# A fused attention and mixture-of-experts kernel: attention and experts put into one block, the top-k cut into two halves of 8 batches, and the first expert's weights and first chunk placed inside the last attention passes

## The reference

```python
q = layernorm(x) @ Wq.T; k = ctx @ Wk.T; v = ctx @ Wv.T          # 16 heads of 16
y = softmax(mask(q k^T / 4)) v                                    # causal
x = x + tanh(g_xattn) * (y @ Wo.T + bo)

affinity = softmax(x @ gate_w.T)             # [16, 512, 8 experts]
gating, idx = top_k(affinity^T, 128)         # per batch and expert: 128 of 512 tokens
x_in = x[idx]
h = silu(x_in @ w_gate[e].T) * (x_in @ w_up[e].T)
out = scatter_add(zeros, idx, gating * (h @ w_down[e].T))
x = x + tanh(g_ffn) * out
```

## Time and profile before

| | us |
|---|---|
| median of 3 runs | 1907.35 (1906.61 to 1908.03) |
| the profiled execution's own time | 1905.62 |
| its span (first to last instruction) | 1903.9 |
| start of body 15 (last batch's maxima) to last maximum | 751.87 to 794.9 |
| last maximum to `aff` of batch 15 (the drain) | 794.9 to 844.06 |
| `aff` to the first matmul of the experts | 844.06 to 874.69 |
| first matmul of chunk 3 of expert 0 | 969.09 |
| last matmul | 1891.7 |
| busy share of PE, DVE, ACT, POOL | 93%, 57%, 49%, 49% |

### The profile page before, as it was taken

The page is one execution under the profiler, slowest core; times in us unless marked ns, Lnnn a source line. Parts: engine busy times, 40 slices in busy tenths (PEclk is TensorE's granted clock), DMA queues, the critical chain, the costliest instruction groups (busy, mean ns, idle before and its releaser), DMA issues.

```text
span 1903.9 us, 40685 instructions
## 1 busy us (share of the span) xinstructions
PE 1772.4 (93%) x12902; PEld 1017.8 (53%) x12902; DVE 1079.0 (57%) x3480; ACT 930.5 (49%) x1812; POOL 931.3 (49%) x1026
## 2 busy tenths in 40 slices
PE   3899999999999999935899999999899999999997
PEld 1355555555555555422465656565556565656565
DVE  2778888888888887737634343434343434343431
ACT  2466666666666666632334343434343434343332
POOL 6477777777777776543333232333322323333322
PEclk8899999999999999967999999999999999999999
DMA  5777777777777787347464644556736555555222
GB/s 161 163 172 188 189 188 188 188 188 188 188 188 188 188 189 168 81 132 177 100 132 84 120 98 89 98 90 122 123 61 121 100 89 98 89 97 82 48 34 23
DMA packets 408333, 247.85 MB, mean 130 GB/s; under 512 B 289303, under 2 KB 389759, under 8 KB 408191
## 3 DMA queue, kind: packets, MB, share of 16 engines
q1 hardware_dynamic: 383183, 212.39, 47.7%
q0 software_dynamic: 24576, 33.57, 11.3%
q10 hardware_dynamic: 432, 0.13, 0.0%
HBM read 118.63 MB, written 58.72 MB: 93 GB/s over the span
## 4 chain that ended last, share of the span: by engine, by line
PE 50%; DVE 3%; DMA 1%; issue 1%; ACT 0%; POOL 0%; SPq 0%; POOLq 0%; DVEq 0%
PE bank L1101 11%; PE bank L1102 11%; PE bank L1103 11%; PE bank L1117 6%; PE bank L1119 6%; PE bank L1118 6%; DVE h L1219 0%; DVE h L1222 0%; DVE top_at L1169 0%; ACT h L1147 0%; DVE work L1172 0%; DVE top L1167 0%; DMA rows<-tokens,row_now 0%; DMA out<-y,row_now 0%; POOL out L1067 0%
## 5 line engine op out<-in xcount | busy, mean ns | idle before, releaser
L1067 POOL DMA_INDIRECT out<-y,row_now x128 | 202.5, 1582 | 606.6 <-ACT y L1154 581.7
L681 DVE CUSTOM_DVE_ANT_0 masked<-bank,causal 128x128 bf16<-128x128 f32 (+3 forms) x1024 | 445.6, 484 | 69.1 <-PE bank L453 68.2
L565 ACT ACTIVATE prob<-bank 128x512 f32<-128x512 f32 x640 | 367.6, 596 | 158.1 <-PE bank L473 86.1
L1219 DVE TENSOR_TENSOR h<-bank,silu 128x512 f32<-128x512 f32 x256 | 176.4, 689 | 393.5 <-PE bank L1103 259.8
L1147 ACT ACTIVATE h<-h 128x512 bf16<-128x512 f32 x256 | 161.2, 630 | 345.4 <-DVE h L1219 328.5
L1117 PE MATMUL bank<-downT,h 128*128 128x256 bf16 x1024 | 279.1, 273 | 0.0
L1119 PE MATMUL bank<-downT,h 128*128 128x256 bf16 x1024 | 279.1, 273 | 0.0
L1118 PE MATMUL bank<-downT,h 128*128 128x256 bf16 x1024 | 279.1, 273 | 0.0
L1222 DVE TENSOR_TENSOR h<-h 128x512 bf16<-128x512 f32 x256 | 177.3, 692 | 179.7 <-ACT h L1147 175.5
L453 PE MATMUL bank<-ks,qs 96*128 96x128 bf16 (+3 forms) x1024 | 257.8, 306 | 21.0 <-DMA ks<-k_parts 11.4
L1101 PE MATMUL bank<-tokT,gateT 128*128 128x512 bf16 x512 | 195.0, 381 | 35.7 <-DMA tokT<-rows 28.9
(11 more groups left out here) (141 smaller groups left out, 2702.7 us busy)
## 6 DMA issues: line engine op xcount, KB each, us to landing
...
```

Of the source, the lines that this page charges most:

```text
L565: nc.scalar.activation(prob[:, gr % 2, h0:h0 + nh, POFF[tiles[0]]:POFF[tiles[0]] + w], sc_bank[SC_BANK[k]][:, 0:nh * w].rearrange("p (h w) ...
L681: last = nc.vector.tensor_tensor_reduce(masked[:, (gr * NMAX + k) % 2, part], max_bank[max_at(gr, k)][:, part], causal[:, T - w:T], 1.0, L ...
L1067: nc.gpsimd.indirect_dma_start(out_rows, bass.IndirectOffsetOnAxis(ap=row_now[:, par, c, s:s + 1], axis=0), y[:, c % 2, s, :], None, compu ...
```

## The change

Both parts are put into one block. Buffers are laid out by hand in four regions of SBUF; buffers of the experts lie where attention's inputs, scores and drain buffers were, and waits on the counters of attention (`finished`) stand ahead of their first use. The steps of attention's last bodies carry steps of expert 0 (table `AHEAD`): each engine runs them at that group and unit.

The ranks of a chunk are now 64 of 8 batches instead of 32 of all 16: chunks 0 and 1 take batches 0 to 7 (**half** 0), chunks 2 and 3 batches 8 to 15 (half 1). The top-k of a half is 64 rows of 8 batches by 8 experts, which DVE first copies twice side by side (`two`) so that PE's transposes (`rows`) fill all 128 partitions; `copied` brings them to `work`. Each half has its own 16 rounds on a 128x512 tile, 32 in all. A slice covers 64 ranks.

In the last bodies stand: the load of expert 0's gate and up weights at the start of body 15, with the splits through bodies 15 and 16 and the transposes; rounds 0 to 3 of half 0 in body 15, rounds 4 to 15 in body 16, with two slices, eight gathers and eight token transposes in bodies 16 and 17; and the eight `up` iterations of chunk 0 from late in body 16 to body 17. What follows is `first_expert`: chunks 1 to 3 of expert 0 with the whole top-k of half 1 in chunks 1 and 2, and the first weights of expert 1, whose low parts POOL now computes (`lo_on_pool`). The token transposes of chunks 2 and 3 now stand at the end of the list of the chunk ahead, behind the weights of its iteration 7.

```diff
+AHEAD = {
+    (LAST - 1, 0, 8): e0("two", 0), (LAST - 1, 1, 3): e0("rows", 0) + e0("copied", 0),
+    (LAST, 0, 0): e0("load", 0, "gate") + e0("load", 0, "up") + e0("base", 0),
+    (LAST, 0, 6): e0("round", 0, 0), (LAST, 1, 6): e0("round", 0, 1),
+    (LAST, 2, 6): e0("round", 0, 2), (LAST, 3, 6): e0("round", 0, 3),
+    (LAST, 1, 0): e0("weights", 0, 0), (LAST, 1, 4): e0("weights", 0, 1), (LAST, 1, 8): e0("weights", 0, 2),
+    (LAST, 2, 1): e0("weights", 0, 3), (LAST, 2, 5): e0("weights", 0, 4), (LAST, 2, 9): e0("weights", 0, 5),
+    (LAST, 3, 2): e0("weights", 0, 6), (LAST, 3, 5): e0("weights", 0, 7),
+    (LAST, 3, 0): e0("turn", 0, "gate"), (LAST + 1, 0, 3): e0("turn", 0, "up"),
+    (LAST + 1, 0, 1): e0("round", 0, 4), (LAST + 1, 0, 4): e0("round", 0, 5),
+    (LAST + 1, 0, 7): e0("round", 0, 6), (LAST + 1, 0, 9): e0("round", 0, 7),
+    (LAST + 1, 0, 10): e0("slice", 0) + e0("columns", 0) + [p for s in range(4) for p in e0("gather", 0, s)],
+    (LAST + 1, 1, 6): [p for s in range(4) for p in e0("tok", 0, s)],
+    (LAST + 1, 1, 1): e0("round", 0, 8), (LAST + 1, 1, 5): e0("round", 0, 9), (LAST + 1, 1, 9): e0("round", 0, 10),
+    (LAST + 1, 2, 3): e0("round", 0, 11), (LAST + 1, 2, 7): e0("round", 0, 12), (LAST + 1, 3, 1): e0("round", 0, 13),
+    (LAST + 1, 3, 4): e0("round", 0, 14), (LAST + 1, 3, 7): e0("round", 0, 15),
+    (LAST + 1, 3, 9): e0("slice", 1) + e0("columns", 1) + [p for s in range(4) for p in e0("gather", 1, s)],
+    (LAST + 2, 1, 5): [p for s in range(4) for p in e0("tok", 1, s)],
+    (LAST + 1, 2, 10): e0("load", 0, "down") + [("load", 1, 1, 0, "gate"), ("load", 1, 1, 0, "up")],
+    (LAST + 1, 3, 2): e0("up", 0, 1) + e0("weights", 0, 8), (LAST + 1, 2, 9): e0("up", 0, 0),
+    (LAST + 1, 3, 5): e0("up", 0, 2) + e0("weights", 0, 9), (LAST + 1, 3, 8): e0("up", 0, 3) + e0("weights", 0, 10),
+    (LAST + 1, 3, 10): e0("weights", 0, 11),
+    (LAST + 2, 0, 1): e0("up", 0, 4) + e0("turn", 0, "down") + [("load", 1, 1, 0, "down")], (LAST + 2, 0, 5): e0("up", 0, 5),
+    (LAST + 2, 0, 9): e0("up", 0, 6), (LAST + 2, 1, 4): e0("up", 0, 7),
+}
 
...
+    def lo_on_pool(e):
+        return isinstance(e, int) and e < 2
+
+    def first_expert():
+
+        order = []
+        for c in range(1, CHUNKS):
+            for it in range(IT):
+                if (c, it) in ((2, 6), (3, 0)):
+                    order += [("columns", 1, 1, c - 2)] + [("gather", 1, 1, c - 2, s) for s in range(CHUNK)]
+                order.append(("up", 0, 0, c, it))
+                if c == 1:
+                    order += {0: [("two", 0, 0, 1), ("rows", 0, 0, 1), ("copied", 0, 0, 1)],
+                              1: [("round", 0, 0, 1, 0), ("round", 0, 0, 1, 1)], 2: [("round", 0, 0, 1, 2), ("round", 0, 0, 1, 3)],
+                              3: [("round", 0, 0, 1, 4), ("round", 0, 0, 1, 5)], 4: [("round", 0, 0, 1, 6), ("round", 0, 0, 1, 7)],
+                              5: [("round", 0, 0, 1, 8)], 6: [("round", 0, 0, 1, 9)], 7: [("round", 0, 0, 1, 10)]}[it]
+                if c == 2 and it < 5:
+                    order.append(("round", 0, 0, 1, 11 + it))
+                if (c, it) in ((1, 4), (2, 4)):
+                    order += [("slice", 0, 0, c + 1), ("columns", 0, 0, c + 1)] + [("gather", 0, 0, c + 1, s) for s in range(CHUNK)]
+                if it % 2 == 1:
+                    order.append(("weights", 1, 1, 0, 4 * (c - 1) + it // 2))
+                if c == 3 and it % 2 == 0:
+                    order.append(("tok", 1, 1, 0, it // 2))
+                order += {(2, 3): [("load", 2, 0, 0, "gate")], (3, 1): [("load", 2, 0, 0, "up")]}.get((c, it), [])
+            if c < 3:
+                order += [("tok", 0, 0, c + 1, s) for s in range(CHUNK)]
+            else:
+                order.append(("load", 2, 0, 0, "down"))
+            order += [("down", 0, 0, c - 1, s) for s in range(CHUNK)]
+        return order
...
```

More of the change, by code:

```diff
@@ L1 @@
+import math
 from contextlib import ExitStack
@@ L304, in rounds_apart, with rows_bank @@
                 body(b, p)
+    def rows_bank(b, half):
+        order = steps(b)
+        jobs = [q for q in steps(b - 1) + order[:order.index(("expert", b, ("rows", 0, 0, half)))] if starts_job(q)]
+        mine = 1 - JOB_BANK[key(jobs[-1])]
+        q = [q for q in jobs if JOB_BANK[key(q)] == mine][-1]
+        return job_bank[mine], mine, (read[q[0]], count(q[1], JOBS_A_BATCH[q[0]], key(q)[1] + 1))
     def free_bank(pe, b, p):
@@ L912, in experts @@
[L912 to L919 removed]
+    work = sb(KEEP, "work", [P, T], F32)
+    two = sb(KEEP, "two", [P, NT, 2, P // 2], F32)
@@ L946, in schedule @@
                 last = (e, par, c - 1) if c else (e - 1, 1 - par, CHUNKS - 1)
[L947 to L949 removed]
+                order += [("columns", *aft)] + [("gather", *aft, s) for s in range(CHUNK)]
                 for it in range(IT):
                     order.append(("up", e, par, c, it))
[L952 to L953 removed]
                     if it in (0, 2, 4, 6):
@@ L959, in schedule, with run @@
                         order.append(("load", e + 2, par, 0, PARTS[c - 1]))
-                if later:
-                    order += [("slice", *aft), ("columns", *aft)] + [("gather", *aft, s) for s in range(CHUNK)]
                 order += [("down", *last, s) for s in range(CHUNK)]
         return [p for p in order if not isinstance(p[1], int) or 0 <= p[1] < EXPERTS]
-    def run(eng, piece, first, final):
-        for p in first:
-            piece(p)
+    def run(eng, piece):
         for p in schedule(0):
@@ L974, in run, with finished, rows_bank @@
             piece(p)
-        for p in final:
-            piece(p)
-    BEFORE = ([("load", 0, 0, 0, n) for n in PARTS] + [("weights", 0, 0, 0, k) for k in range(8)]
-              + [("round", 0, 0, 0, r) for r in range(PER_CHUNK)] + [("slice", 0, 0, 0), ("columns", 0, 0, 0)]
-              + [("gather", 0, 0, 0, s) for s in range(CHUNK)] + [("tok", 0, 0, 0, s) for s in range(CHUNK)]
-              + [("weights", 0, 0, 0, k) for k in range(8, WJOBS)] + [("load", 1, 1, 0, n) for n in PARTS]
-              + [("round", 0, 0, 1, r) for r in range(PER_CHUNK, 2 * PER_CHUNK)]
-              + [("slice", 0, 0, 1), ("columns", 0, 0, 1)] + [("gather", 0, 0, 1, s) for s in range(CHUNK)])
-    AFTER = [("down", EXPERTS - 1, 1, CHUNKS - 1, s) for s in range(CHUNK)]
+        for s in range(CHUNK):
+            piece(("down", EXPERTS - 1, 1, CHUNKS - 1, s))
+    def finished(eng, *what):
+        for n in what:
+            s, per = att["done"][n]
+            eng.wait_ge(s, BATCH * per)
+    g["link"]["rows_copied"] = S["rows_copied"]
+    def rows_bank(half):
+        return att["rows_bank"](LAST - 1, 0) if half == 0 else (g["job_bank"][0], 0, (att["done"]["aff"][0], BATCH))
     def weights_raw(k):
```

1694 lines of the change are left out of this document (906 added, 788 removed).

## The result

The changed kernel took **1942.56 us** (median of 5 runs, 1939.54 to 1947.09) against 1907.35 us (1905.86 to 1908.39): a ratio of 1.0187, 95% interval 1.0172 to 1.0202, 35 us slower. The profiled execution had a span of 1940.8 us against 1903.9, 36.9 us more. The stretches of the view of busy time show where it went. Columns: the stretch, its length, then busy time and instructions of PE, PE's weight loads, DVE, ACT, POOL, then PE's granted clock, DMA share and GB/s.

A forecast was written before the change was run, and what follows sets the result against it. PE bounds the kernel (busy 93%), with a DVE chain at the seam between attention and experts. T moves by +32 us, T to chunk 3 by −11.7: 1907.35+20.3 = about 1927 us; range 1902 to 1944.

The forecast's parts named there:

- rival C: PE at half clock in the drain: chunk 0's matmuls take 41 us, T at most 16 us later, 1943 us; chance 0.12.
- the forecast's own unknowns: Step 1 ±4, slices −1 to +6, drain's waits −7 to +5, SP holds ±4: about 1912 to 1940 us.
- Step 1: Bodies 14 and 15: four added rounds, `two` and `copied` on DVE cost 6 us (2.3 to 10.5); weight splits cost nothing.
- The rounds' term: Four top-k rounds added in body 15: 9.3 us on DVE, against 8.2 us of DVE idle time there.
- Step 2: Drain, last maximum to T (`aff` of batch 15): 45.8 us of added DVE work makes it 74.3 us, not 49.2: +25.1.
- A chain, not room: Drain: DVE's 36.7 us idle cannot cover added work, since its waits are for PE, which waits for DVE's last result.
- its own sign of being wrong: Drain: the prediction is wrong if DVE shows 20 us or more of idle time there.
- The table loads: ACT switches between exponentials and silu five times instead of once: four more of 1.28 us, 5.1, mostly hidden, +1 taken.
- Step 3: T to chunk 3 of expert 0: 113.3 us against 125.0, −11.7, with chunks 2 and 3 held by SP's weight transposes.
- A: Token transposes follow their gather, not held by weights: chunk 3 starts at T+92, 33 us earlier than before, 1906; chance 0.15.
- B: The drain hides the added DVE work: it lengthens by 4 us, T moves by 6, not 32, 1902; chance 0.15.
- D: POOL's subtractions delay DVE casts or h subtractions in chunks 1 and 2: 0 to 9 us; chance 0.10.

## Why the prediction was right in direction and short by 15 us

The measured 1942.6 lies in the stated range of 1902 to 1944, and that is luck: the upper end was drawn for rival C, which is not what happened, and the forecast's own unknowns ended at 1940 (its terms add up to 1927.7).

- **Step 1, bodies 14 and 15: wrong.** The text put 6 us (2.3 to 10.5) on it; it was 18.0. It counted DVE's rounds, put the weight splits at nothing and left out what else moves there: the two loads of 1 MB on SP's queue. Body 15's 15.2 us divide by the runs into 6.3 for the loads (58.2 to 51.9; 3.4 to 6.3 by all profiles), 7.5 for the four rounds (52.1 to 44.6) and 1.6 that stay. The rounds' term was 4.8 of 9.3, with about half of DVE's idle time as cover; they were covered by 1.8. The other 2.8 come ahead of body 15: 2.1 in body 14 with `two` and `copied` (48.7 us from its start to body 15's, 46.6 before), where 1.2 was allowed, and 0.7 before that.
- **Step 2, the drain: right.** 25.1 and 1 were said, 26.3 came. DVE's list with its 8.8 us wait at the end is what the view by line shows; the two slices took 1.6 and 2.6 us instead of 1.35 each, the waits a little more or less than allowed, place by place. (Two rounds, not three, stand between the last maximum and the first residual.) Once the list is full, more work costs its length: the run with four more rounds in the drain (8.8 us more for 9.3 of rounds) shows it directly. "A chain, not room" is too strong, though. The walk itself let 45.8 us of work lengthen the drain by 25.1, and without chunk 0 17.6 of 28.0 us fitted into idle time. And by its own sign of being wrong, 20 us or more of idle DVE time in the drain, the walk would have failed: 24.3 us were idle. The sign was set too low, since the walk's own waits (6.8, 9.4 and the pairs' eight of 0.6) come to some 21.
- **The table loads: right in number,** five from body 15 on; their 5.1 us stand beside DVE's work, and no run separates them from the h pairs.
- **Step 3, T to chunk 3: right in mechanism, 4.5 us short.** Chunk 2 started at T+62.4 (T+59.5 said), chunk 3 at T+116.0 (T+111.5 said), with PE waits of 11.5 and 14.2 us (10 and 13 said). The size missed on the weight transposes, 6.7 and 6.6 us instead of 4.6 and 5.5, and on two h subtractions (below). The swap on SP's list shows that the order there is the cause.
- **The rivals.** A became true as soon as SP's list was changed, at T+89.6 instead of T+92. B is refuted by the drain's 75.5 us. C did not decide, and that its 1943 is what was measured is chance: the drain's granted clock was 0.84, higher than the 0.79 before, PE's busy time there grew by 19.5 us, about the 20.8 of an up pass at full clock, and DVE's list was the longer one. The clock can still be worth some 4 us in the drain, as the same instructions at 0.84 and 0.81 show. D is there and is worth 1.5 us of DVE's time behind T. The loads that delay a small transfer, up to 6.3 of the missing 12 us, were in no rival; the rest are the rounds' cover (2.7) and small terms.
- **The rule on the exclusive port.** The Trainium skill ("SBUF — State Buffer", Who interferes with whom) says that a DVE instruction with two inputs in SBUF contends with a GpSimd instruction that reads SBUF. The trace now agrees for the h subtraction too: DVE's timeline of the changed kernel has

```profile
925.83 0.69 DVE L1423 TENSOR_TENSOR h<-h,h 128x512 bf16<-128x512 f32 x1 [0.70 <-ACT h L1331]
...
930.14 1.46 DVE L1423 TENSOR_TENSOR h<-h,h 128x512 bf16<-128x512 f32 x1 [0.69 <-ACT h L1331]
```

where the second lies over POOL's subtraction

```profile
929.88 1.17 POOL L1206 TENSOR_TENSOR gate_nat<-gate_raw,gate_nat 128x512 bf16<-128x512 f32 x1
```

It takes 1.46 us instead of 0.69; the other such case is at 983.27 (1.44). Subtractions that began ahead of POOL's, as at 911.02 and 935.21, took 0.69. The MAX8 rows stay at about 0.69 throughout.

So the change loses in three ways. It gives DVE 16 more rounds (27 us by the run that leaves them out), it puts weights ahead of tokens on SP's list (27.8 us by the swap; the two overlap by some 8 us of waits), and it places half 0's rounds and chunk 0 in front of the steps that end attention, where DVE's list is the path. What it wins is smaller: chunk 0 ahead of T (8 us), weights ahead of T (8 us, of which 6.2 or, placed better, 2.5 are paid ahead of T). The weights alone, without the halves, win 0.2 to 0.3%.
